# A rotary embedding whose two products both come from PSUM, with the swap after the sine product and the sum on GpSimd

## The reference

```python
def _rope(x):                         # x: tokens x heads x 128
    even, odd = jnp.split(x, 2, axis=-1)
    return concatenate([even * cos - odd * sin, even * sin + odd * cos], axis=-1)

q = _rope(einsum('btm,mhd->bthd', x, w_aq))
k = _rope(einsum('btm,mhd->bthd', x, w_ak))
v = einsum('btm,mhd->bthd', x, w_av)
s = einsum('bihd,bjhd->bhij', q, k) / 128 - 1e30 * (i < j)
r = einsum('bihd,hdm->bim', einsum('bhij,bjhd->bihd', softmax(s), v), w_ao)
x = layernorm(x + r)
h = silu(lin(x, w1)) * lin(x, w2); h = gelu(lin(h, h1)); h = gelu(lin(h, h2))
x = layernorm(x + lin(h, w3))
```

## Time and profile before

| | value |
|---|---|
| median of three runs | 1079.12 us |
| profiled execution | 1077.77 us, of which the span is 1076.0 us |
| busy over the span | PE 93%, PEld 80%, DVE 79%, ACT 61%, POOL 54% |
| mean granted clock of PE | 0.979 of full speed |
| attention, from the start to | about 785 us |
| feed-forward and norms | the rest |
| DMAs `swapped<-proj` | 256, of 128 KB, median 2.3 us from issue to landing |

### The profile page before, as it was taken

The page is one execution under the profiler, slowest core; times in us unless marked ns, Lnnn a source line. Parts: engine busy times, 40 slices in busy tenths (PEclk is TensorE's granted clock), DMA queues, the critical chain, the costliest instruction groups (busy, mean ns, idle before and its releaser), DMA issues. The chain is left out here.

```text
span 1076.0 us, 20027 instructions
## 1 busy us (share of the span) xinstructions
PE 995.9 (93%) x5648; PEld 859.3 (80%) x5648; DVE 852.0 (79%) x1803; ACT 655.7 (61%) x1383; POOL 584.5 (54%) x536
## 2 busy tenths in 40 slices
PE   2799999999999999999999999999839999999995
PEld 1588888888888888888888888888728878788784
DVE  4888888988889898888888888888755668486744
ACT  4577676777767677777767777777625252343531
POOL 3777777777777877767787777777350101000000
PEclk8799999999999999999999999999969999999998
DMA  7542223432223223232222222221020000000000
GB/s 249 167 137 60 69 61 88 153 89 59 60 69 73 63 58 91 58 77 64 76 49 58 60 60 70 69 68 40 1 79 1 1 1 21 0 19 0 1 20 20
DMA packets 33292, 66.16 MB, mean 61 GB/s; under 512 B 5456, under 2 KB 6992, under 8 KB 32208
## 3 DMA queue, kind: packets, MB, share of 16 engines
q1 hardware_dynamic: 30400, 58.62, 20.6%
q10 hardware_dynamic: 2832, 6.82, 1.7%
HBM read 24.26 MB, written 7.34 MB: 29 GB/s over the span
## 5 line engine op out<-in xcount | busy, mean ns | idle before, releaser
L720 POOL TENSOR_SCALAR probs<-probs,inv_sum 128x128 f32<-128x128 f32 (+7 forms) x256 | 236.7, 925 | 173.5 <-DVE inv_sum L635 173.5
L537 ACT ACTIVATE pT<-psum 128x512 fp32r<-128x512 f32 (+3 forms) x384 | 176.0, 490 | 131.2 <-PE psum L404 130.1
L311 PE MATMUL psum<-pT,vals 128*128 128x512 f32 (+3 forms) x1152 | 242.2, 350 | 1.6 <-DVE rT L678 1.6
L525 ACT ACTIVATE probs<-psum,neg_max 128x128 f32<-128x128 f32 (+7 forms) x256 | 190.3, 744 | 48.8 <-DVE neg_max L629 46.9
L645 DVE TENSOR_TENSOR pT<-psum,pT 128x512 fp32r<-128x512 f32 (+3 forms) x384 | 199.8, 547 | 14.8 <-ACT pT L537 11.8
L311 PEld LDWEIGHTS psum<-pT,vals 128*128 128x128 f32 x1152 | 187.3, 189 | 24.0 <-DVE pT L645 1.7
L629 DVE TENSOR_REDUCE neg_max<-psum 128x1 f32<-128x128 f32 (+7 forms) x256 | 190.4, 744 | 3.7 <-PE psum L395 3.7
L404 PE MATMUL psum<-ident,probs 128*128 128x128 f32 x1152 | 174.6, 276 | 12.8 <-POOL probs L720 6.4
L725 POOL TENSOR_TENSOR swapped<-swapped,rope 128x512 f32<-128x512 f32 x128 | 165.4, 1292 | 37.2 <-DMA swapped<-proj 37.1
L901 PE MATMUL ps<-hid,w 128*128 128x512 f32 x768 | 181.3, 396 | 0.0
L901 PEld LDWEIGHTS ps<-hid,w 128*128 128x128 f32 x768 | 143.8, 188 | 34.4
(11 more groups left out here) (78 smaller groups left out, 1267.9 us busy)
## 6 DMA issues: line engine op xcount, KB each, us to landing
swapped<-proj SPq DMA_DIRECT2D x256, 128.0 KB, 2.3
w_stage<-qk_split SPq DMA_DIRECT2D x30, 256.0 KB, 2.6
wv_stage<-v_split SPq DMA_DIRECT2D x15, 256.0 KB, 2.6
x_split<-ffn_raw ACTq DMA_DIRECT2D x2, 1024.0 KB, 5.9
ffn_raw<-g SPq DMA_DIRECT2D x2, 1024.0 KB, 8.1
x_moving<-x_split SPq DMA_DIRECT2D x2, 1024.0 KB, 5.9
out<-y SPq DMA_DIRECT2D x4, 512.0 KB, 2.6
raw_x<-xT SPq DMA_DIRECT2D x3, 512.0 KB, 11.5
```

What stands on the lines that cost most here:

```text
L311: ins = nc.tensor.matmul(out_ap, left[a], right[b], start=first and i == 0, stop=last and i == 2)
L525: nc.scalar.activation(probs[:, ib % 4, :width].rearrange("p (h c) -> p h c", h=halves), score_ps[:, ib % 2, :halves, :half], ACT.Exp, bia ...
L537: nc.scalar.activation(pT[chunk][:, 0, 4 * f:4 * f + n_blocks, (ib % 4) * P:(ib % 4 + 1) * P], bank("t", head[1], nth)[:, :n_blocks * P].r ...
L720: nc.gpsimd.tensor_scalar(p, p, inv_sum[:, n:n + 1], 1.0, ALU.mult, ALU.mult).then_inc(probs_ready[0], 1)
```

## The change

The copy to `proj` on ACT goes. DVE now makes both products of a tile from PSUM, first the sine product into `by_sin` (two buffers), then the cosine product into `by_cos` (`rope_products`). The DMA swaps the halves of the sine product instead of those of the projection, so the table of sines changes its sign pattern. POOL adds `swapped` and `by_cos` (`rope_sum` moves from DVE to POOL). The step tables change: sums at steps 2, 2, 4, 5, high parts at 3, 3, 5, 6, low parts at 3, 4, 6, 7; the cosine and sine tables are gone, and the products follow `QK_STEP`, two tiles per step as the projections are. `QK_STEP` itself and the bank plan stay, and with them PE's order.

```diff
--- before.py
+++ after.py
@@ -48,11 +48,9 @@
 
 
 QK_STEP = (0, 0, 2, 2)
-COS_STEP = (0, 0, 2, 2)
-SIN_STEP = (1, 2, 3, 4)
-SUM_STEP = (2, 3, 4, 6)
-HIGH_STEP = (3, 4, 6, 8)
-LOW_STEP = (3, 4, 6, 8)
+SUM_STEP = (2, 2, 4, 5)
+HIGH_STEP = (3, 3, 5, 6)
+LOW_STEP = (3, 4, 6, 7)
 V_STEP = (4, 5, 6, 6)
 PV0_PIECES = {6: range(0, 2), 7: range(2, 4)}
 PV1_PIECES = {1: range(0, 2), 2: range(2, 4), 3: range(4, 8)}
@@ -130,7 +128,7 @@
     wv_stage = sb("wv_stage", [P, 2, 2 * P], F32R)
     x_moving = sb("x_moving", [P, 2, 2, T], F32R)
     qk = sb("qk", [P, 2, 2, 2, T], F32R)
-    proj = sb("proj", [P, 2, BANK])
+    by_sin = sb("by_sin", [P, 2, BANK])
     by_cos = sb("by_cos", [P, NQK, BANK])
     swapped = sb("swapped", [P, NQK, BANK])
 
@@ -180,7 +178,6 @@
     t_high = (sem("t_high"), NT)
     t_low = (sem("t_low"), NT)
     qk_projected = (sem("qk_projected"), NQK)
-    proj_copied = (sem("proj_copied"), 4)
     cos_done = (sem("cos_done"), 4)
     sin_done = (sem("sin_done"), 4)
     rope_done = (sem("rope_done"), 4)
@@ -353,9 +350,9 @@
                     if q == 0 and not first:
                         stage_for_values()
                     for j in range(NQK):
-                        wait_for(sp, proj_copied, head, j)
+                        wait_for(sp, sin_done, head, j)
                         for lo, hi in ((0, 64), (64, 0)):
-                            sp.dma_start(swapped[lo:lo + 64, j], proj[hi:hi + 64, j % 2]).then_inc(
+                            sp.dma_start(swapped[lo:lo + 64, j], by_sin[hi:hi + 64, j % 2]).then_inc(
                                 swap_done[j % 2][0], 16)
                     if q == 0 and first:
                         stage_for_values()
@@ -538,15 +535,6 @@
                         pT[chunk][:, 0, 4 * f:4 * f + n_blocks, (ib % 4) * P:(ib % 4 + 1) * P],
                         bank("t", head[1], nth)[:, :n_blocks * P].rearrange("p (j i) -> p j i", i=P),
                         ACT.Copy).then_inc(t_high[0], 1)
-
-            def copy_projected(head, j):
-                wait_for(act, qk_projected, head, j)
-                old_head, old = earlier(head, j, 2, 4)
-                wait_for_swap(act, old_head, old)
-                wait_for(act, rope_low, step_on(head, -1), j)
-
-                nc.scalar.activation(proj[:, j % 2], bank("qk", 1 if parity(head) else 2, j),
-                                     ACT.Copy).then_inc(proj_copied[0], 1)
 
             def roped_high(head, j):
                 which, c = ROPE_TILES[j]
@@ -589,8 +577,6 @@
                     roped_high(target, j)
                 if exists(head):
                     transposed_high(head, s)
-                for target, j in rope_tasks(head, s, QK_STEP):
-                    copy_projected(target, j)
                 for c in v_tasks(head, s):
                     values_high(head[0], c)
 
@@ -646,18 +632,17 @@
                         low, bank("t", head[1], nth)[:, :n_blocks * P].rearrange("p (j i) -> p j i", i=P),
                         high.bitcast(F32), ALU.subtract).then_inc(t_low[0], 1)
 
-            def times_cos(head, j):
+            def rope_products(head, j):
                 c = ROPE_TILES[j][1]
-                wait_for(dve, proj_copied, head, j)
-                wait_for(dve, rope_done, step_on(head, -1), j)
-                nc.vector.tensor_tensor(by_cos[:, j], bank("qk", 1 if parity(head) else 2, j),
-                                        rope[:, 0, c * BANK:(c + 1) * BANK],
+                projected = bank("qk", 1 if parity(head) else 2, j)
+                old_head, old = earlier(head, j, 2, 4)
+                wait_for(dve, qk_projected, head, j)
+                wait_for_swap(dve, old_head, old)
+                wait_for(dve, rope_low, step_on(head, -1), j)
+                nc.vector.tensor_tensor(by_sin[:, j % 2], projected, rope[:, 1, c * BANK:(c + 1) * BANK],
+                                        ALU.mult).then_inc(sin_done[0], 1)
+                nc.vector.tensor_tensor(by_cos[:, j], projected, rope[:, 0, c * BANK:(c + 1) * BANK],
                                         ALU.mult).then_inc(cos_done[0], 1)
-
-            def rope_sum(head, j):
-                wait_for(dve, sin_done, head, j)
-                wait_for(dve, cos_done, head, j)
-                nc.vector.tensor_tensor(swapped[:, j], by_cos[:, j], swapped[:, j], ALU.add).then_inc(rope_done[0], 1)
 
             def values_low(pair, nth):
                 high, low = (vals[:, part, 2 * nth:2 * nth + 2].rearrange("p j q m -> p (j q m)") for part in range(2))
@@ -689,8 +674,6 @@
                         low_of_x(b)
                 if exists(step_on(head, (s + 1) // NI)):
                     inverse_sum(step_on(head, (s + 1) // NI), (s + 1) % NI)
-                for target, j in rope_tasks(head, s, SUM_STEP):
-                    rope_sum(target, j)
                 if exists(step_on(head, (s + 2) // NI)):
                     negative_max(step_on(head, (s + 2) // NI), (s + 2) % NI)
                 if s == ADD0_STEP:
@@ -699,8 +682,8 @@
                     add_head(step_on(head, -1), 1)
                 if exists(head):
                     transposed_low(head, s)
-                for target, j in rope_tasks(head, s, COS_STEP):
-                    times_cos(target, j)
+                for target, j in rope_tasks(head, s, QK_STEP):
+                    rope_products(target, j)
                 for c in v_tasks(head, s):
                     values_low(head[0], c)
 
@@ -719,11 +702,10 @@
                 p = probs[:, ib % 4, :(ib + 1) * P]
                 nc.gpsimd.tensor_scalar(p, p, inv_sum[:, n:n + 1], 1.0, ALU.mult, ALU.mult).then_inc(probs_ready[0], 1)
 
-            def times_sin(head, j):
-                c = ROPE_TILES[j][1]
+            def rope_sum(head, j):
                 wait_for_swap(pool, head, j)
-                nc.gpsimd.tensor_tensor(swapped[:, j], swapped[:, j], rope[:, 1, c * BANK:(c + 1) * BANK],
-                                        ALU.mult).then_inc(sin_done[0], 1)
+                wait_for(pool, cos_done, head, j)
+                nc.gpsimd.tensor_tensor(swapped[:, j], by_cos[:, j], swapped[:, j], ALU.add).then_inc(rope_done[0], 1)
 
             def roped_low(head, j):
                 which, c = ROPE_TILES[j]
@@ -735,8 +717,8 @@
                 ahead = step_on(head, (s + 1) // NI)
                 if exists(ahead):
                     normalize(ahead, (s + 1) % NI)
-                for target, j in rope_tasks(head, s, SIN_STEP):
-                    times_sin(target, j)
+                for target, j in rope_tasks(head, s, SUM_STEP):
+                    rope_sum(target, j)
                 for target, j in rope_tasks(head, s, LOW_STEP):
                     roped_low(target, j)
 
@@ -1168,7 +1150,7 @@
     freq = np.power(np.float32(10000.0), -np.arange(half, dtype=np.float32) / np.float32(half)).astype(np.float32)
     angle = (np.arange(T, dtype=np.float32)[None, :] * freq[:, None]).astype(np.float32).astype(np.float64)
     cos, sin = np.cos(angle), np.sin(angle)
-    rope = np.stack([np.concatenate([cos, cos]), np.concatenate([-sin, sin])], axis=1).astype(np.float32)
+    rope = np.stack([np.concatenate([cos, cos]), np.concatenate([sin, -sin])], axis=1).astype(np.float32)
 
     def by_tile(a, tiles):
         return a.T.reshape(tiles, P, -1).transpose(1, 0, 2).reshape(P, -1)
```

## The result

The changed kernel takes 1066.04 us as a median (1065.0 to 1066.31), the kernel before 1079.03 us (1076.83 to 1079.99) in the same comparison. The ratio is 0.9879, with a 95% interval of 0.9862 to 0.9895: 13.0 us faster. Forecast were 1073 us and 6 us less. The span of the profiled executions goes from 1076.0 to 1064.2, and the changed one's own time, 1065.99, is its median; 1.2 of the 13.0 us are thus the distance of the profiled execution of before from its median.

What follows compares the result with a forecast made beforehand. PE's instruction stream was taken as the unchanged bound, so only PE's standstills could be won. Steady +0.8, start -3.7, head 0 -1.5, first heads of a batch -1.9 sum to -6.3 us: 1073 us from 1079.1, range 1060 to 1086.

Steps and rivals of the forecast that it cites:

- Start and head 0: Kernel start: first scores near 25.5 instead of 29.28, gain 3.7 us; head 0: DVE's removed sum frees the max, gain 1.5.
- First heads of a batch: Three such heads and their neighbours: DVE's removed sum no longer holds the max, gain 1.9 us.
- Steady stage: 15 pairs of heads: odd head gains 0.15 us, even head loses 0.2, in sum +0.8 us.
- The odd head's walk: Odd head: 0.4 us stop at block 4's scores, block 6's max unmoved, shorter normalisation before block 7's transposes; gain 0.15 us.
- the others shrink: Odd head: the 0.93 us stop before block 0's scores goes; those at blocks 5 and 6's transposes get shorter.
- POOL's and ACT's new order: End of odd head: 0.1 us taken off the 0.28 us won on the normalisation.
- The even head's walk: Even head: block 2's reciprocal slips, so its transposes start at 460.1 instead of 459.93; 0.2 us lost.
- the three gaps of the earlier trace: Odd head: PE stops of 0.48, 0.93, 0.40 us at block 5's transposes, block 0's scores, block 6's transposes; 1.81 per pair.
- POOL's slow passes: POOL's normalisations beside DVE's sum: 512 columns regain 0.5 us at block 3, 1024 columns 0.28, without that sum.
- Rival 1: Steps 0 to 2 of each head: DVE's block of products becomes the bound, 1091 us, 1085 likelier; chance 0.24.
- Rival 2: Pairs and start: all three stops vanish as normalisations and maxes come sooner, 32 us faster, 1047 us; chance 0.10.
- 1.29 us earlier: POOL's queue from step 3 on: one operation less before tile 1's low part, which comes 1.29 us earlier.

Runs made afterwards that it cites:

- experiment three: Changed kernel plus four idle 512-column copies per head on ACT: 1065.86 us, ratio 0.9879 to the kernel before.
- experiment four: Changed kernel with one more 512-column product on DVE in each block of four: 1084.49 us, ratio 1.0052 to the kernel before.
- experiment eight: Changed kernel with DVE's second `add_head` of a head moved ahead of block 6's maximum: 1062.01 us, ratio 0.9846 to the kernel before.
- experiment one: Changed kernel with the step tables of before, sums still on POOL: 1075.64 us, ratio 0.9964 to the kernel before.
- experiment nine: Kernel before with earlier steps for the later tiles alone, sum on DVE, sine product on POOL, copies on ACT: 1112.02 us, ratio 1.0320.
- five: Changed kernel with only tile 1's sum and high part one step later, as before: 1065.52 us, ratio 0.9874 to the kernel before.
- two: Changed kernel with the step tables of before and the sum back on DVE: 1075.34 us, ratio 0.9963 to the kernel before.
- experiment six: Changed kernel with tile 1's sum and high part one step later and the sum back on DVE: 1088.6 us, ratio 1.0092 to the kernel before.

## Why the prediction was wrong

The direction was right and the range held the time, but the gain is twice the forecast. Step by step:

**Start and head 0: right in sum, and that in part by luck.** -3.7 and -1.5 were forecast, together -5.2; the mark of head 0 moved by -4.9. The first scores came 0.7 us earlier than the 25.5 written down: there POOL's second and third operations were charged with x subtractions beside them, and are 1.26 us each. PE then stops again, and block 2's scores come at 31.05 instead of 33.94, so the start gave 2.9 us, and head 0 up to its mark 2.0. What the forecast left out is that POOL's sums now lie beside DVE's three x subtractions: these last 6.7 us from start to end (23.42 to 30.13) instead of 4.6, and the first maximum comes at 30.05 instead of the forecast 29.1. The gap at 51.04 in the earlier trace rows is gone: the same transposes start at 46.24 without one.

**First heads of a batch: too large.** -1.9 was forecast. The gap at 284.90 is gone; by the marks that row lies in the second pair of the second batch, not in its first. The 15 periods fall by 7.0 us: three of them by 0.78 to 0.93 (the one that ends at 284.96 and two about the start of the last batch), the other twelve by 0.26 to 0.47, 0.38 in the mean. Taken as 15 x 0.38, the steady stage gives 5.7 us, and 1.4 is left for this term.

**Steady stage: the step that failed.** It had +0.8 us and came out at -5.7. The forecast took -0.15 per odd head and +0.2 per even head; the pair shown here gave -0.42 (46.56 to 46.14 from block 2's scores to block 2's scores). From scores of block 2 to scores of block 2, the timeline of PE before is

```profile
454.33 0.39 PE L391 MATMUL psum<-qk 128*128 128x384 f32 x1
...
478.38 0.39 PE L391 MATMUL psum<-qk 128*128 128x384 f32 x1
...
500.89 0.39 PE L391 MATMUL psum<-qk 128*128 128x384 f32 x1
```

and after

```profile
445.65 0.39 PE L388 MATMUL psum<-qk 128*128 128x384 f32 x1
...
491.79 0.39 PE L388 MATMUL psum<-qk 128*128 128x384 f32 x1
```

with 469.59 shown above. Odd head: 22.51 to 22.20, -0.31. Even head: 24.05 to 23.94, -0.11.

*The odd head's walk was right up to its last part.* The new stop at block 4 is there (0.21 us between starts, forecast 0.4, because DVE reaches the products 0.18 us sooner after block 2's scores). Block 6's scores end 0.34 us later against block 2's (forecast 0.4), and the maximum stands at 14.07 us behind block 2's scores where it stood at 14.08: "The max starts when it did" held to 0.01 us. From that maximum to block 7's transposes it was 6.91 us and is 6.57. Its three parts are these: from the maximum to the normalisation 5.30 and now 5.32 us, the normalisation 1.40 and 1.12, from its end to the transposes 0.21 and 0.13. The forecast took 0.1 off for "POOL's and ACT's new order", but the first part shows that this order costs next to nothing, and the third part was not in the forecast. Error: 0.16 per pair. One thing the text had otherwise: of the three stops "the others shrink", but the one at block 6's transposes grew from 0.40 to 0.79 us. PE waits for the chain there first, and only 0.26 us at block 7.

*The even head's walk stopped too early.* What the forecast said of block 2's transposes, "start at 460.1: 0.2 us lost", is right: they stand 5.74 us behind block 2's scores instead of 5.60, and block 6's scores are 0.22 us late in all. But the text ended there, and the even head of before had two more stops that the three gaps of the earlier trace rows do not hold:

```profile
470.73 0.64 PEld L404 LDWEIGHTS psum<-ident,probs 128*128 128x128 f32 x6 [0.38 <-DVE pT L645]
...
471.52 0.77 PEld L311 LDWEIGHTS psum<-wv_stage,x_moving 128*128 128x128 f32 x6 [0.16 <-DVE vals L665]
```

Both are ended by DVE work that stood behind the maximum of block 6. That one started at 468.40, 1.27 us after the second group of its scores at 467.13, and DVE had not been idle before it. After, it starts at 459.60, 0.93 us after that group at 458.67 and after 1.53 us of waiting for it, and neither stop is there: 3.60 to 3.48 us from scores to transposes, and 0.79 to 0.59 from transposes to the projections of v. Together -0.32 where nothing was counted. Error: 0.31 per pair, the larger one. The two make 0.47 us in this pair, 7.1 us if all 15 were like it. The distance between forecast and measurement is 6.5 us (+0.8 to -5.7), since not every pair is: the even head's first stop stands in 11 of them.

The list of waits of before, 60 to 780 us, told of it:

```profile
PEld psum L404 <- DVE pT L645: 12.4, 26, 1.0
```

26 places are more than 15 odd heads account for: 11 lie in even heads, at the transposes of block 5 as in the row at 470.73. I walked only the odd head's gaps.

**Terms that held.** ACT's copies are worth nothing (experiment three). SP's DMAs are not on the path. POOL's slow passes go as said, and of the 0.5 us at block 3 no PE stop tells. Rival 1 (DVE's block as bound) did not come, but it was close: experiment four shows that one more product in step 0 reaches PE whole, so the slack of about 1.2 us from which this rival was to decide isn't there for work of that step. Rival 2 did not come: PE's stops for the chain through block 7 remain, and experiment eight, which shortens that chain, is faster.

**What the change needed.** The forecast treated the tables as a detail ("1.29 us earlier"). With the tables of before the same arithmetic is worth 0.36% or 3.6 us (experiment one), all of it at the start, and with the new ones 13; in the kernel before the new ones cost 33 (experiment nine). The new steps of the later tiles pay with the sum on POOL (10 us between experiments one and five) and cost with it on DVE (13 us between two and six).

**The port that DVE and POOL share.** In the earlier trace rows a sum that starts at 490.82 lasts until 492.54, 0.55 us beyond the end of POOL's two-input operation beside it (490.70 to 491.99). In experiment six it is the other way: the sum starts first and takes 0.67 us, and POOL's pass is longer by 0.25. Whoever starts later pays. The Trainium skill (SBUF — State Buffer, section "SBUF: two separate sides") says that such a DVE operation and a GpSimd operation that reads SBUF exclude each other; the trace agrees, but for 0.13 to 0.14 us: a sum held until 491.99 would end at 492.67, and a pass held until 311.09 would end at 312.10 where it ends at 311.96. What remains open is how the 23 us of experiment six divide between this and DVE's own time, and why each pair of experiment nine loses 1.7 us at full clock, more than either theory had.

## What to carry to other kernels

Walk every head of a repeating unit to its end, from the list of waits: each releaser's count there says how many stops per unit there must be, and a walk that accounts for fewer has left one out. Here the 0.21 us that PE lost at block 4 did not delay block 6's maximum, which stood behind DVE's own sum before and now waits for PE; what was won at the end of the odd head was won on the chain of DVE, ACT and POOL. Before an operation is moved to another queue, look at what stands behind it there at each step: here the arithmetic alone gave 3.6 us, the same with the later tiles' work earlier 13.

## What the runs showed of the hardware

A DVE addition of 512 columns with two SBUF inputs takes 0.685 us in the mean where it starts before POOL's operation (experiment six); where it starts behind one it took 1.42 us (experiment nine) and 1.72 us. POOL's scaling of 896 columns takes 1.015 us by itself, 1.265 behind the start of such an addition, and up to 1.46. At the start of the changed kernel the x subtractions, 1.21 us at the least in the kernel before, take 2.07 to 2.30 us beside POOL's sums and low parts, and two of these take 2.26 and 2.24 us instead of 1.26. DVE's products with one input from PSUM have means of 0.678 to 0.684 us in all kernels here, and POOL's addition with two SBUF inputs 1.29.

PE's granted clock fell to 0.50 (1.2 GHz) in experiment nine, four times between 60 and 740 us; one fall, at 323 us, came after 5 us in which PE was busy for 2.9, and the clock was still 0.50 up to 326 us. Two of the four odd heads in which it fell have a longer stop at block 5's transposes than the rest (0.93 us against 0.33 to 0.59), the other two do not; what decides it is not shown. In all other kernels here its mean from 60 to 740 us is 1.00.
